# A gated delta-rule layer on one Trainium2 core: half of a projection, a decay's Exp and a shift moved within the order of a group

## The reference

```python
qkvz = x @ W_qkvz                       # 16 groups of q, k (128), v, z (2 x 128)
qkv = silu(causal_conv1d(qkv, conv_weight))        # 4 taps
g = -exp(A_log) * softplus(a + dt_bias)            # per value head and token
# per head, in chunks:
decay_mask = exp(clip(g[:, None] - g[None, :], -30, 30)) * tril
attn = -(k_beta @ k.T * decay_mask), strictly lower; then forward substitution, + eye
value_corrected = attn @ v_beta;  k_cumdecay = attn @ (k_beta * g_exp)
# chunk after chunk:
v_prime = v_c - k_cumdecay_c @ state
out = (q_c @ state) * g_exp + (q_c @ k_c.T * decay_mask) @ v_prime
state = state * g_last + (k_c * k_decay).T @ v_prime
out = rmsnorm(out * silu(z)) @ W_out
```

## Time and profile before

| | |
|---|---|
| runs | 1745.14, 1734.08, 1746.89 us; median 1745.14 |
| the profiled execution's own time | 1761.52 us |
| its span | 1759.8 us |
| mean granted clock of TensorE | 0.905 |
| the sixteen turns of the delta layer | from about 595 to 1620 us of the span |

### The profile page before, as it was taken

The page is one execution under the profiler, slowest core; times in us unless marked ns, Lnnn a source line. Parts: engine busy times, 40 slices in busy tenths (PEclk is TensorE's granted clock), DMA queues, the critical chain, the costliest instruction groups (busy, mean ns, idle before and its releaser), DMA issues. The chain is left out here.

```text
span 1759.8 us, 38626 instructions
## 1 busy us (share of the span) xinstructions
PE 1443.5 (82%) x14345; PEld 1032.2 (59%) x14345; DVE 1135.3 (65%) x2336; ACT 852.7 (48%) x2401; POOL 781.1 (44%) x1116
## 2 busy tenths in 40 slices
PE   5988982378624798999999999999999999986665
PEld 2543341245412466677677677777767767775465
DVE  5885138622456576787786787787778778743623
ACT  2335851132113555656655656766665665643122
POOL 6000000465201464665555555666467556453343
PEclk9999995588867898999999999999999999978688
DMA  8100005165613534645555555554464554432783
GB/s 284 54 2 2 1 4 147 31 195 166 216 53 71 129 93 124 161 117 150 142 150 117 140 151 120 151 160 113 140 173 119 152 149 127 107 92 76 202 266 126
DMA packets 249435, 218.74 MB, mean 124 GB/s; under 512 B 88770, under 2 KB 224962, under 8 KB 247200
## 3 DMA queue, kind: packets, MB, share of 16 engines
q1 hardware_dynamic: 234992, 192.41, 39.8%
q0 software_dynamic: 5712, 15.60, 2.7%
q10 hardware_dynamic: 8544, 8.26, 1.5%
HBM read 133.85 MB, written 82.25 MB: 123 GB/s over the span
## 5 line engine op out<-in xcount | busy, mean ns | idle before, releaser
L1674 PE MATMUL d_big<-all_xn_t,all_w 128*128 128x512 f32 x512 | 264.2, 649 | 27.8 <-DVE d_conv L1892 21.4
L1892 DVE SCALAR_TENSOR_TENSOR d_conv<-d_big,all_cw,d_conv 128x1023 f32<-128x1023 f32 (+2 forms) x192 | 245.4, 1278 | 48.0 <-ACT d_conv L2056 45.6
L2242 POOL TENSOR_TENSOR d_y<-d_y,all_xn 128x256 f32<-128x256 f32 x128 | 96.0, 750 | 183.6 <-DVE d_y L2033 153.2
L1674 PEld LDWEIGHTS d_big<-all_xn_t,all_w 128*128 128x128 f32 x512 | 98.3, 207 | 119.6 <-issue 97.0
L2156 ACT COPY d_ys<-d_big 128x128 f32<-128x128 f32 x256 | 61.0, 267 | 198.2 <-PE d_big L1825 139.1
L1863 PE MATMUL d_big<-all_wo,d_yt 128*128 128x256 f32 x512 | 125.7, 391 | 13.7 <-DVE d_yt L1962 13.7
L1796 PE MATMUL d_big<-all_w,all_xn_t 128*128 128x256 f32 x512 | 126.0, 390 | 0.0
L1936 DVE SCALAR_TENSOR_TENSOR d_AI<-d_big,d_b_col,d_decay 128x256 f32<-128x256 f32 x256 | 105.7, 474 | 27.0 <-PE d_big L1687 23.4
L1863 PEld LDWEIGHTS d_big<-all_wo,d_yt 128*128 128x128 f32 x512 | 96.9, 197 | 26.2 <-issue 14.2
L1796 PEld LDWEIGHTS d_big<-all_w,all_xn_t 128*128 128x128 f32 x512 | 94.5, 192 | 18.9 <-issue 7.2
L347 DVE TENSOR_REDUCE a_neg_max<-a_big 128x1 f32<-128x128 f32 (+7 forms) x128 | 90.3, 751 | 12.9 <-PE a_big L276 12.8
(11 more groups left out here) (443 smaller groups left out, 3513.7 us busy)
## 6 DMA issues: line engine op xcount, KB each, us to landing
turned_kq_scratch<-d_turned SPq DMA_DIRECT2D x32, 512.0 KB
d_kq_tok<-turned_kq_scratch SPq DMA_DIRECT2D x128, 128.0 KB
turned_v_scratch<-d_vs SPq DMA_DIRECT2D x16, 1024.0 KB
d_vs<-turned_v_scratch SPq DMA_DIRECT2D x64, 256.0 KB
grouped_y_scratch<-d_yx SPq DMA_DIRECT2D x32, 512.0 KB
d_yx<-grouped_y_scratch SPq DMA_DIRECT2D x128, 128.0 KB
all_w<-in_L_attn_W_qkvz SPq DMA_DIRECT2D x16, 768.0 KB
l_hold<-in_L_ffn_gate_up_proj SPq DMA_DIRECT2D x48, 192.0 KB
```

Of the source, the lines that this page charges most:

```text
L1674: mm = pe.matmul(big[0][:, c, :], w_sb[par][:, k, n * DK:(n + 1) * DK], xn_t[:, k, c * 512:(c + 1) * 512], start=(k == 0), stop=(k == KD - 1))
L1892: dve.scalar_tensor_tensor(conv[:, sh:T], src[:, 0:T - sh], cw[:, bass.ds(g, 1), COLUMN_OF[j], 3 - sh], conv[:, sh:T], ALU.mult, ALU.add). ...
L2242: pool.tensor_tensor(part, part, zs[:, t, :], ALU.mult).then_inc(s["yg_s"], 1)
```

## The change

Three of the tables are edited; no instruction is added, removed or altered.

```diff
 PE_ORDER
-    ... gates 3; prev iv 7; this l1p 0, l1p 1, l1p 2, l1p 3; next proj 2
-    0, proj 2 1; this l1y 0, ...
+    ... gates 3; prev iv 7; next proj 2 0; this l1p 0, l1p 1, l1p 2, l1p 3;
+    next proj 2 1; this l1y 0, ...
 DVE_ORDER
-    ... this v_turn 1; next tap 0 1, tap 0 2, tap 0 3; this qe; next
-    kq_turn 0; prev gather 6; this l0p; next shift, tap 1 1, ...
-    this l1p; prev y_turn 0; next kb; this l1y; next products 0; this l2p; next products 1; this l2y; ...
+    ... this v_turn 1; next shift, tap 0 1, tap 0 2, tap 0 3; this qe; next
+    kq_turn 0; prev gather 6; this l0p; next tap 1 1, ...
+    this l1p; prev y_turn 0; next kb; this l1y, l2p; next products 0, products 1; this l2y; ...
 ACT_ORDER
-    this gates 1; prev sq2 4, o1 7; next tap0 1; prev sq2 5; this gates 2, l0y; next silu 1, ksq 0, ksq 1, ksq 2; this
-    l1p; next ksq 3, decay; this gates 3, l1y, l2p; prev sq2 6, sq2 7; ...
+    this gates 1; next decay; prev o1 7; next tap0 1; prev sq2 4, sq2 5; this gates 2, l0y; next silu 1; this gates 3; next ksq 0, ksq 1; this
+    l1p; next ksq 2, ksq 3; this l1y, l2p; prev sq2 6, sq2 7; ...
```

More of the change, by code:

```diff
@@ L1397 @@
     0, l0p 1, l0p 2, l0p 3, l0p 4; next proj 1 0; this l0p 5, l0p 6, l0p 7; prev qs 7; next proj 1 1; this l0y 0, l0y 1,
-    l0y 2, gates 2, l0y 3, l0y 4, l0y 5, l0y 6, l0y 7, gates 3; prev iv 7; this l1p 0, l1p 1, l1p 2, l1p 3; next proj 2
-    0, proj 2 1; this l1y 0, l1y 1, l1y 2, l1y 3; next products 0; this l2p 0, l2p 1; next products 1, products 2; this
+    l0y 2, gates 2, l0y 3, l0y 4, l0y 5, l0y 6, l0y 7, gates 3; prev iv 7; next proj 2 0; this l1p 0, l1p 1, l1p 2, l1p 3;
+    next proj 2 1; this l1y 0, l1y 1, l1y 2, l1y 3; next products 0; this l2p 0, l2p 1; next products 1, products 2; this
     l2y 0, l2y 1; next products 3; this y 0, kv 0, iv 0, ks 1; prev out_mm 0 0; this y 1, qs 1, kv 1, iv 1, ks 2, qs 2;
@@ L1405 @@
 DVE_ORDER = steps_of("""
-    prev state 6; this v_turn 0; prev r 7, gather 5; this v_turn 1; next tap 0 1, tap 0 2, tap 0 3; this qe; next
-    kq_turn 0; prev gather 6; this l0p; next shift, tap 1 1, tap 1 2, tap 1 3; prev gather 7; this l0x; next kq_turn 1;
-    this l1p; prev y_turn 0; next kb; this l1y; next products 0; this l2p; next products 1; this l2y; next products 2;
+    prev state 6; this v_turn 0; prev r 7, gather 5; this v_turn 1; next shift, tap 0 1, tap 0 2, tap 0 3; this qe; next
+    kq_turn 0; prev gather 6; this l0p; next tap 1 1, tap 1 2, tap 1 3; prev gather 7; this l0x; next kq_turn 1;
+    this l1p; prev y_turn 0; next kb; this l1y, l2p; next products 0, products 1; this l2y; next products 2;
     this state 0, gather 0, r 1; next products 3; this state 1, gather 1; next tap 2 1; this r 2; next tap 2 2; this
@@ L1416 @@
     prev sq2 0, o1 5, sq2 1, ys 6, sq2 2, sq2 3; this silu 3; next tap0 0; this gates 0; prev ys 7, o1 6; next silu 0;
-    this gates 1; prev sq2 4, o1 7; next tap0 1; prev sq2 5; this gates 2, l0y; next silu 1, ksq 0, ksq 1, ksq 2; this
-    l1p; next ksq 3, decay; this gates 3, l1y, l2p; prev sq2 6, sq2 7; this l2y, ys 0; next tap0 2; this ys 1, o1 1;
+    this gates 1; next decay; prev o1 7; next tap0 1; prev sq2 4, sq2 5; this gates 2, l0y; next silu 1; this gates 3; next ksq 0, ksq 1; this
+    l1p; next ksq 2, ksq 3; this l1y, l2p; prev sq2 6, sq2 7; this l2y, ys 0; next tap0 2; this ys 1, o1 1;
     next qsq 0; this ys 2, o1 2, ys 3, o1 3; next silu 2, qsq 1; this ys 4; next tap0 3; this o1 4, ys 5
```

## The result

The changed kernel takes 1816.43 us (median of 4 runs, 1812.32 to 1821.26) against 1739.61 (4 runs, 1732.61 to 1746.89): a ratio of 1.044, 95% interval 1.038 to 1.051, slower by 77 us. Run again later, with the experiments, it is 1.0445 (1.036 to 1.053). The forecast was 1770, 1.5% slower; its range ended at 1796. The profiled execution took 1821.26 us.

A forecast was written before the change was run, and what follows sets the result against it. A group was taken to cost what TensorE executes plus its waits plus the clock's loss. +22 us of waits over fifteen turns and +4 of clock gave +26 on the median 1745.1, said as 1770; range 1742 to 1796.

The forecast's parts named there:

- Of the 1.90 us about 0.1 is left: TensorE's wait ahead of L1735: the half projection moved there fills it, a gain of 1.8 us a group.
- that the clock doesn't explain: 8 us of the 35 above fourteen clean groups, booked as waits inside L1749 and L1752 in a few groups.
- The shift takes 1.60 us in the median: Shift ahead of the taps: fills VectorE's 0.74 us wait, makes TensorE wait 0.86 us (0.5 to 1.9) at projection 1.
- TensorE waits 0.9 us: Ahead of L1749: TensorE waits 0.9 us a group for ScalarE's negation L2111.
- the drain: About 1380 ns after ScalarE's table load: not counted; it would lengthen the chain 2.8 us, the time to about 1813.
- Waits 1.05 us ahead of L1769: TensorE waits 1.05 us a group for VectorE's L1991, behind small norm operations (0.78 us) that need all eight squares.
- 0.45 us: At product 2: TensorE waits 0.45 us a group for VectorE's first four products, now behind L1996.
- The sum, +1.5 us a group or 63.4: The waits of a clean group added up: about +1.5 us, a period near 63.4 us, +22 us over fifteen turns.
- 31 against the 27 that go: Clock from L1769 through L1687: falls in 12 of 15 groups at 2.6 us, 31 against 27 saved: +4 us.
- The direction: The whole kernel was forecast slower, at chance 0.66, against same 0.27 and faster 0.07.
- the clock falls in every group: Rival: the clock falls everywhere and longer, through L1781, 58 us against 27, time 1798; chance 0.20.
- the clock holds: Rival: the two short waits near L1749 leave the clock up, 27 us return against +22, time 1740; chance 0.22.

The follow-up runs named there:

- e16: The changed kernel with v_in issued one step later, behind kq_out 1, and GpSimd's two large multiplications replaced by constant writes: 0.9995 of the kernel before.
- e5: The changed kernel with GpSimd's two large multiplications (L2265, L2199) replaced by constant writes: 1.0202 of the kernel before.
- e11: The changed kernel with the return transfer v_in issued one step later, behind kq_out 1, and nothing else: 1.0150 of the kernel before.
- e12: The changed kernel itself, run again with the experiments: 1.0445 of the kernel before.
- e8: The kernel before with only VectorE's l2p copy moved ahead of the product 0 evacuation: 1.0064 of the kernel before.
- e1: The kernel before with only TensorE's edit, half of projection 2 ahead of L1735: 1.0226 of the kernel before.
- e10: Kernel before with TensorE's edit, v and output return transfers cut to a quarter of their rows, GpSimd's scaling of v a constant write: 1699.6 us, 0.979.
- e1 to e4: Parts of the change: TensorE's edit, 1.0226; shift alone, 1.0118; ScalarE's order and shift, 1.0256; changed kernel with ScalarE's old order, 1.0333.

## Why the prediction was wrong, step by step

- "Of the 1.90 us about 0.1 is left": right for the wait, nothing in most groups and 0.18 us in five. Wrong in what it said is late next. The step took the second sweep as ready to run as soon as L2111 was there. The kernel before had stops in L1749 and L1752 by "issue", and the prediction booked them as 8 us "that the clock doesn't explain" and left them as they were. They were TensorE's instruction reads behind the bulk transfers, and the wait that went away had been their cover. This is the missing term: 36 us with the clock behind it by e16 against e5, and 51 by e11 against e12, where hold-ups of L1911 went too.
- "The shift takes 1.60 us in the median, 1.22 to 2.62 ... 0.86 us (0.5 to 1.9 by the two ends)": the place was right, the size was no middle. In its new place it is 1.18 us (mostly 0.30 of wait at projection 1, less than forecast) or 2.6 to 2.9 (1.5 to 2.0 of wait, the upper end), by whether GpSimd's L2265 started first. That the fifteen waits add up to 14.7 us, near the forecast's 13, is chance. The 2.62 in the earlier trace rows was the sign of it, with GpSimd's L2281 beside it, and the 1.60 of the median was one too: in ten of the sixteen GpSimd's L2242 (0.73 us) had started 0.2 us before. No row of GpSimd was laid beside the shift. Nor did the step ask what the shift itself waits for: at the start of the layer that is another 8.3 us, which the sum put at nothing.
- "TensorE waits 0.9 us" at L1749: 0.79 in nine groups, 0.30 in four. Right. It also decides about the drain that the Trainium skill (ScalarE: Activation LUTs, "What ACT_TABLE_LOAD costs") adds to a load, which would have put L2111 some 2.8 us later and the time at 1813: the wait shows no such delay, and e16, with the same order on ScalarE, takes as long as before. That 1813 lies near the measured time is chance.
- "Waits 1.05 us ahead of L1769": 1.04, in fourteen of e16's groups. In the changed kernel up to 3.5, since L1911 stands ahead of L1991 and is held up by L2199 in eight of fifteen groups. The step took the small operations on the norms at 0.78 us, their time of before; ScalarE's later squares pushed them to where L2199 runs.
- "0.45 us" at product 2: 0.48, in most groups of e16. Right; e8 shows it alone, at 0.6%.
- The sum, +1.5 us a group or 63.4: e16's group is 63.30 against the 61.85 of the earlier trace rows, +1.45. It is right by the sum, and in part by luck. By the parts it is 0.30 + 0.79 + 1.04 + 0.48 - 1.8 = 0.8, and TensorE's busy time is 0.64 longer (59.98 against 59.34), which no step had.
- The clock, "31 against the 27 that go", +4 in the sum: this is the term that was off by most. In the changed kernel it is 77, because the stops of 2 to 3 us and the waits of up to 3.5 at L1769 stand among the same small matmuls. Without the two hindrances it is (1 - 0.99) x 888 = 9 in e16: there the first rival, "the clock holds", was right. Fourteen of e16's groups take 13 us less than before (888.32 against 901.34): 14 x 1.45 = 20 more, and 33 less of what stands above fourteen clean groups (35 before, 2 now), of which the clock's 18 and the stops' 8 are known. The start of the layer, up to the first L1735, takes 11 more (85.6 against 74.5), and so the time is that of before (0.9995). This holds with GpSimd's two multiplications left out; the kernel before without them was not run, so what they cost it is not known.
- The direction was right, and for most of it by the wrong reason: by e5 and e16 as much as the whole 77 us came from what the order collides with. The chain that was added up is there, but the clock that comes back without the collisions pays for it. The rival "the clock falls in every group", at 1798, came nearest, for the trace's reason of short stops among small matmuls, but the stops were others.

What stays open: why e1's stops come in nine groups and not in all (in three of the others, and in none of the nine, a read had run 2.9 us ahead of L1736; for the rest no reason was found), what each us of stop costs in clock, since only sums of both were measured, and what e10's and e16's left-out work would be worth in the kernel before.

## What to carry to other kernels

A wait by "issue" in a dense sweep of small matmuls is worth a look at the DMA engines and the instruction queue in the same microseconds: a wait ahead of it may be its cover, and taking that away gains nothing until the bulk transfers are moved too. A duration with a wide spread (1.22 to 2.62) is no distribution to take the middle of; look what GpSimd ran when it was long, and lay the moved instruction over GpSimd's rows as well as over its own engine's. When one of several linked edits loses, take the suspects out of the whole, one and then both, rather than adding the parts up: e5, e11 and e16 settled what e1 to e4 could not. And run the kernel before with the same work left out; without that, what the left-out work is worth stays unknown, as it does here. An instruction that is moved ahead brings its own waits along: look at the start of the loop as well, where its input may not be there yet.
